# Delta-rule stage: the inverse's first products moved ahead of the next group's projections

## The reference, cut to what matters

```python
def step(S, inp):                      # one token, S is 32x32 for each head
    q_t, k_t, v_t, b_t = inp
    pred = jnp.einsum('bhk,bhkv->bhv', k_t, S)
    err = (v_t - pred) * b_t[..., None]
    S = S + jnp.einsum('bhk,bhv->bhkv', k_t, err)
    o_t = jnp.einsum('bhk,bhkv->bhv', q_t, S)
    return (S, o_t)
...
q = _l2norm(split(x @ Wq, Dk)); k = _l2norm(split(x @ Wk, Dk)); v = split(x @ Wv, Dv)
beta = jax.nn.sigmoid(x @ Wbeta).transpose(0, 2, 1)
o = _delta_rule(q, k, v, beta)
o = o * jax.lax.rsqrt(jnp.mean(o * o, axis=-1, keepdims=True) + RMS_EPS) * g_norm
return o.transpose(0, 2, 1, 3).reshape(B, N, H * Dv) @ Wo
```

## Time and profile before

| what | value |
|---|---|
| median of three runs | 4267.09 us (4266.0 to 4274.78) |
| the profiled execution | 4268.37 us, of which the span 4266.6 us |
| PE busy | 3884.7 us, 91% of the span |
| DVE busy | 3266.5 us, 77% |
| ACT busy | 3119.9 us, 73% |
| POOL busy | 1511.8 us, 35% |
| mean granted TensorE clock | 0.951 of full speed |
| chain that ended last | PE 59%, ACT 18%, DVE 14%, issue 6%, POOL 3% |

### The profile page before, as it was taken

One profiled execution on the slowest core, in us unless ns is written; L12 is line 12 of the kernel. 1 busy time (PEld: TensorE's weight loads), 2 busy tenths in 40 slices (PEclk: granted clock), 3 DMA queues, 4 the chain that ended last, 5 costly groups with the idle time before them and its releaser, 6 DMA issues.

```text
span 4266.6 us, 58145 instructions
## 1 busy us (share of the span) xinstructions
PE 3884.7 (91%) x15924; PEld 2177.6 (51%) x15924; DVE 3266.5 (77%) x10600; ACT 3119.9 (73%) x5775; POOL 1511.8 (35%) x2843
## 2 busy tenths in 40 slices
PE   6799789999999999999999999998699669999976
PEld 4567634444444444444444444443366447777755
DVE  6877588888888888888888888886667766666668
ACT  3555369999999999999999999998243436666654
POOL 2331234444444444444444444443211114333320
PEclk8888799999999999999999999999799879999988
DMA  2122010000000000000100000000000001111100
GB/s 61 31 45 40 7 25 1 15 11 1 20 6 1 20 6 1 20 6 1 23 3 8 18 1 16 11 1 1 0 1 1 0 15 46 46 45 43 43 7 20
DMA packets 151990, 71.08 MB, mean 17 GB/s; under 512 B 109577, under 2 KB 142685, under 8 KB 151667
## 3 DMA queue, kind: packets, MB, share of 16 engines
q1 hardware_dynamic: 144738, 63.96, 5.8%
q10 hardware_dynamic: 6928, 3.41, 0.3%
HBM read 54.55 MB, written 12.80 MB: 16 GB/s over the span
## 4 chain that ended last, share of the span: by engine, by line
PE 59%; ACT 18%; DVE 14%; issue 6%; POOL 3%; DMA 0%; DVEq 0%; SPq 0%; ACTq 0%; POOLq 0%
PE bank L2093 16%; PE bank L2883 5%; PE bank L2108 5%; PE bank L2137 5%; ACT arena L2185 3%; PE bank L2916 3%; PE bank L2147 3%; ACT arena L2184 2%; ACT arena L2188 2%; ACT arena L2197 2%; DVE arena L2274 2%; ACT L2231 2%; PE bank L620 2%; PE bank L2943 1%; DVE arena L2297 1%
## 5 line engine op out<-in xcount | busy, mean ns | idle before, releaser
L2093 PE MATMUL bank<-arena 128*128 128x512 f32 x3072 | 1413.5, 593 | 3.9 <-DMA arena<-in_L_attn_Wv_dram 3.7
L2093 PEld LDWEIGHTS bank<-arena 128*128 128x128 f32 x3072 | 584.0, 190 | 739.9 <-issue 719.3
L2334 POOL TENSOR_SCALAR arena<-arena 128x256 f32<-128x256 f32 x1024 | 481.1, 481 | 1156.3 <-DVE arena L2267 1156.3
L2108 PE MATMUL bank<-arena 128*128 128x512 f32 x1024 | 524.5, 604 | 49.6 <-DVE arena L2297 49.6
L2256 DVE SCALAR_TENSOR_TENSOR arena<-arena 128x256 f32<-128x256 f32 x1024 | 393.7, 421 | 184.9 <-ACT arena L2185 176.5
L2297 DVE SCALAR_TENSOR_TENSOR arena<-arena 128x256 f32<-128x256 f32 x1024 | 491.7, 524 | 13.6 <-issue 13.6
L2274 DVE SCALAR_TENSOR_TENSOR arena<-bank,bv,arena 128x256 f32<-128x256 f32 x1024 | 444.7, 472 | 0.0
L2184 ACT ACTIVATE arena<-bank,bqk 128x512 f32<-128x512 f32 x512 | 348.5, 681 | 76.8 <-PE bank L2093 72.5
L2267 DVE SCALAR_TENSOR_TENSOR arena<-bank,bq,arena 128x512 f32<-128x512 f32 x512 | 384.1, 750 | 18.0
L2197 ACT ACTIVATE arena<-arena,const_table 128x512 f32<-128x512 f32 x512 | 374.7, 732 | 0.0
L2188 ACT ACTIVATE arena<-bank,bqk 128x512 f32<-128x512 f32 x512 | 354.3, 692 | 0.4 <-PE bank L2093 0.4
(11 more groups left out here) (396 smaller groups left out, 7056.3 us busy)
## 6 DMA issues: line engine op xcount, KB each, us to landing
arena<-packed_dram SPq DMA_DIRECT2D x96, 96.0 KB
arena<-packed_dram SPq DMA_DIRECT2D x32, 288.0 KB
arena<-diag_dram SPq DMA_DIRECT2D x16, 256.0 KB, 3.7
arena<-in_L_attn_Wk_dram SPq DMA_DIRECT2D x16, 256.0 KB, 3.2
arena<-in_L_attn_Wq_dram SPq DMA_DIRECT2D x16, 256.0 KB, 4.0
arena<-in_L_attn_Wv_dram SPq DMA_DIRECT2D x16, 256.0 KB, 4.2
arena<-in_L_attn_Wo_dram SPq DMA_DIRECT2D x8, 512.0 KB, 4.1
arena<-in_L_attn_W_dram SPq DMA_DIRECT2D x16, 256.0 KB, 2.7
```

The costliest lines, as they stand in the source:

```text
L2093: nc.tensor.matmul(bank[:, RING1[m % 5], :], w1p[k][:, i * P:(i + 1) * P], zT_of(g), start=True, stop=True).then_inc(a1_proj.sem, 1)
L2108: nc.tensor.matmul(bank[:, 6, :], wo1[:, i, :], a1_att[:, i % 4, :], start=(i == 0), stop=(i == NB1 - 1)).then_inc(a1_outd.sem, 1)
L2334: last = nc.gpsimd.tensor_scalar(a, a, 1.0, a1_ksum[:, i % 4, b:b + 1], ALU.add, ALU.mult)
```

## The change

Two lists are written in another order; no instruction is added, removed or altered. On PE the two `ax5_pe` stand ahead of `proj_pe`, and `transpose_pe` ahead of the two `rest_pe`. On ACT `spread_act` and the two `x5_act` stand ahead of `keep_act`. DVE, POOL and SP keep their order.

```diff
                 over_slots(
-                    [(3, gram_pe), (1, proj_pe), (2, at_first(turns_pe))] + both(ax5_pe)
+                    [(3, gram_pe)] + both(ax5_pe) + [(1, proj_pe), (2, at_first(turns_pe))]
                     + [(3, i21_pe(0)), (3, it5_pe(0)), (3, i21_pe(1)), (3, it5_pe(1))]
                     + both(x6_pe) + [(4, out_turn_pe)] + both(it6_pe) + [(1, turn_pe), (4, out_pe)]
                     + both(lambda b: err_pe(b, 0)) + [(1, agram_pe)] + both(state_pe)
-                    + both(rest_pe) + [(0, with_parity(transpose_pe))] + both(lambda b: err_pe(b, 1)) + both(o_pe))
+                    + [(0, with_parity(transpose_pe))] + both(rest_pe) + both(lambda b: err_pe(b, 1)) + both(o_pe))
...
                 over_slots(
-                    [(1, keep_act), (2, at_first(turns_act)), (3, spread_act)] + both(x5_act)
+                    [(3, spread_act)] + both(x5_act) + [(1, keep_act), (2, at_first(turns_act))]
                     + [(3, i21_act(0)), (3, it5_act(0)), (3, i21_act(1)), (3, it5_act(1))]
```

## The result

| | before | after |
|---|---|---|
| median, us | 4267.74 (4 runs, 4266.0 to 4274.78) | 4292.72 (4 runs, 4288.15 to 4298.28) |
| ratio to before, 95% interval | | 1.0059 [1.0045, 1.0073] |
| profiled execution, us | 4268.37, span 4266.6 | 4295.33, span 4293.5 |
| mean granted clock | 0.951 | 0.947 |

The change costs 25 us. The forecast had the direction and the mechanism at the head of the slot; the size lay 13 us above it and 3.7 us above the upper end of the range. In the whole page the change is hardly to be seen: PE is at 91% as before, with 17.6 us more busy time in as many instructions.

The account below looks back on a forecast made before the run. The prediction took PE's queue and a DVE and POOL chain, ending together at turn_pe, to bound the slot. Later keeping +11.4, transposes -2.2 and clock +3.2 gave +12.4 us, 4279.5 against 4267.1; 8-in-10 range 4270 to 4289.

Parts of the forecast that it names:

- Two paths end together at `turn_pe`: At turn_pe PE's queue and the DVE and POOL chain arrive together; delaying L1347 delays the slot, 1.62 to 3.06 us.
- term of +11.4 us: Head of slots 3 to 8: summed delay of turn_pe from the last projection tile being kept later, +11.4 us.
- Moving the transposes ahead ... -2.2 us: Ahead of rest_pe: 0.44 us of transposes go into PE's 0.91 us wait in slots 3 to 7, -2.2 us.
- The clock ... I take two, +3.2: PE's stage: two additional falls to 1.2 GHz assumed, +3.2 us, between bounds of 0 and 9.6.
- Rival 3: PE's clock: one more fall per slot, 4286 us, or two in some slots, 4290; chance 0.16.
- Rivals 1, 2 and 4: PE's queue alone decides, 4255 (faster, 0.06); keeping less late, 4271 (0.13); order changes nothing, 4265 to 4267 us (0.07).

Follow-up runs that it names:

- e1: Kernel before with only ax5_pe, spread_act and x5_act moved ahead, transposes left behind rest_pe: 4287.37 us, 1.0041 of the kernel before.
- e4: Changed kernel with POOL's power replaced by a linear instruction: 4279.17 us, 1.0026 of the kernel before.
- e3: Kernel before with POOL's power replaced by a linear instruction: 4261.17 us, 0.9983 of the kernel before.
- e2: Kernel before with only the transposes moved ahead of rest_pe: 4277.62 us, 1.0021 of the kernel before.
- e16: Kernel before with only the transposes moved ahead of rest_pe, run again on another chip: 4284.52 us, 1.0029 of the kernel before.
- e5: Changed kernel with useless wide products in PE's two new waits, in the projections and ahead of turn_pe: 4284.12 us, 1.0035 of the kernel before.
- e11: Kernel before with keeping, sums of squares and power in halves, and unit_dve ahead of exchange_dve: 4274.71 us, 0.9997 of the kernel before.
- e10: Changed kernel with four useless transposes added straight behind rest_pe in slots 3 to 10: 4287.79 us, 1.0029 of the kernel before.
- e14: Changed kernel with four useless transposes added ahead of rest_pe: 4278.78 us, 1.0015 of the kernel before.
- e15: Kernel before with the transposes moved ahead of rest_pe and four useless ones added behind it: 4270.1 us, 0.9998 of the kernel before.
- e9: Kernel before with four useless transposes added behind rest_pe and the real transposes, slots 3 to 10: 4278.82 us, 1.0007 of the kernel before.

## Why the prediction was right or wrong

**Two paths end together at `turn_pe`: right.** L1347 waits for L1342 by 1.34 to 1.42 us in slots 4 to 8, and `turn_pe` is late by 1.39 to 1.45 there (forecast 1.62 to 1.71, since T + 8.30 was measured for T + 8.57). Slot 3 lost 4.01, not 3.06, because of the clock's fall in tiles 2 and 3. The term of +11.4 us measured +11.1; `e1` shows 12.3 for it alone. `e4` bears out that POOL's power is on the path after the change, and `e3` that before it PE's own path was nearly as long. L1329's wait of about 2 us (2.35), the start of L1624 at T + 7.6 (7.33) and a wait at `turn_pe` in each slot (1.27 to 1.89, slot 3 3.00) are there as described.

**"Moving the transposes ahead ... -2.2 us": the step that failed.** Their 0.44 us do lie in the wait, as it said (0.91 to 0.47). The sentence "if that cover were gone they would cost what they cost today" took a product on PE to be worth its own duration. Moving it also changed the clock of the work behind it: in `e2` the ends, with less work in them, ran at 1.2 GHz for 61 us instead of 34 (10 of these 27 us in slot 9). The step was off by 11 to 14 us (-2.2 against the +9 to +12 of `e2` and `e16`). Why the move does this to the clock stays open.

**"The clock ... I take two, +3.2": mis-sized, and looked for in the wrong stretch.** The price of a fall, 1.7 us, was right for the ends too: before the change an end with 3.3 us at 1.2 GHz takes 13.74 us (slot 6) and one with none 12.04 (slot 3). Their number and place were wrong. I looked for falls behind waits, and the head has fewer of them after the change (7.5 us at 1.2 GHz against 13.2). The ends have 27.5 us more at 1.2 GHz, half of it lost, 13.7 us, where 3.2 were booked for the whole stage (13.7 less the 2.2 of moved work is 11.5; the ends grew by 10.3); PE is busy throughout them and no wait takes it up (slot 7, 18.02 us against 13.63). From `turn_pe` to the next T slots 3 to 8 lost 7.4 us where -2.2 and +3.2 were booked, and slot 9, whose order is unchanged and which was booked at nothing, lost 4.4. The Trainium skill, page "TensorE: Matmul & The Clock Gate", section "A second HAM failure mode: psum-queue depth-cycling", says that short idle times of PE between groups of matmuls can swing the clock. `e5` agrees for head and middle, where filled waits took time at 1.2 GHz away; at the end of the slot PE has 0.1 us of idle time in 18 us, and no run here shows whether the rule reaches that.

**The rivals.** Rival 3 (more falls of the clock, 4286 to 4290) came nearest, with a sum about 3 us too small. It put one fall behind a wait in every slot, though, and that is not where they came. Rivals 1, 2 and 4 are out: L1347 waits, and the wait is of nearly the size worked out. What remains open is what makes the clock fall in the end stretches. Which of idle time, width of the products and what went before decides there, these runs don't tell apart.

## What to carry to other kernels

Before a step is put ahead of another to fill a wait, look for who else comes to the consumer: here a chain over DVE and POOL had 0.06 us of slack, and the edit that removed a wait on PE pushed that chain. Where a stage is bound by PE and its products are narrow, compare the time at each clock level by stretch, also in stretches that the edit leaves alone; what such an edit wins in one stretch may be lost in the next. And judge a filled wait by the time of the whole: neither the wait that went (0.44 us here) nor the head's 7.5 us in `e11` was kept.

## What the runs showed of the hardware

- The clock falls while PE is busy. In the end stretch of slot 7 after the change PE was busy 17.92 of 18.02 us, and the clock was 0.62. It fell at about 354.2 us, amid products of 32 columns and 2.9 us after the last listed wait (0.47 us), and rose again at about 367.9 us, amid the grams of 512 columns.
- 3.5 us of products that nobody reads took 13 to 21 us off the changed kernel (0.44 us in each of eight slots; `e10` and `e14` by their ratios against 1.0059 and 1.0064).
- Slots with the same instructions last 42.2 or 46.4 us by turns (slots 4 to 7 after the change), and the end of slot 9 takes 12.0 or 19.95 us with the same ones (`e15`, `e9`), so a single slot read from a trace is no measure of the stage.
- The kernel before varies as well between jobs, 4266.8 to 4274.8 us in the median. Only ratios within a job can be compared here.
